# Layer 1's attention: the last tile's softmax weights made between the two halves of tile 1's value products, and stored and read ahead of the value loads

## The reference, cut to what matters

```python
x = x + jnp.tanh(g_xattn[1]) * _L1_xattn_ref(_layernorm(x, axis=-1), ctx_4096, ...)
# inside: C = 64 channels, 8 heads of depth 8, WINDOW = 16
# q, k, v = pointwise projections; for each t: softmax over 16 shifted keys of q.k / sqrt(8);
# out[t] = sum over the window of weight[t, w] * v[t + shift(w)]; then a pointwise projection
```

## Time and the profile before

| | us |
|---|---|
| median of 3 runs | 2050.9 |
| lowest and highest | 2050.52, 2055.03 |
| the profiled execution, its own time | 2056.09 |
| its span | 2053.9 |
| TensorE busy | 1871.9 (91%) |
| VectorE busy | 1630.7 (79%) |

### The profile page before, as it was taken

One profiled execution on the slowest core, in us unless ns is written; L12 is line 12 of the kernel. 1 busy time (PEld: TensorE's weight loads), 2 busy tenths in 40 slices (PEclk: granted clock), 3 DMA queues, 4 the chain that ended last, 5 costly groups with the idle time before them and its releaser, 6 DMA issues. The chain is left out here.

```text
span 2053.9 us, 37788 instructions
## 1 busy us (share of the span) xinstructions
PE 1871.9 (91%) x15015; PEld 1053.9 (51%) x15165; DVE 1630.7 (79%) x2908; ACT 585.7 (29%) x1347; POOL 655.3 (32%) x786
## 2 busy tenths in 40 slices
PE   8778989889889898998877999999999999999987
PEld 6434565446644456444533455555555555555543
DVE  4689776997679876797745888888888888888885
ACT  2322242223322233222333222222222222222443
POOL 3510242002420114202114544444343434343552
PEclk9899999999899998999988999999999999999997
DMA  8658204461055601463052111111111111111011
GB/s 246 186 157 229 68 2 145 124 190 57 2 165 155 195 2 42 130 195 89 2 179 77 42 32 52 52 52 48 51 42 52 52 52 52 52 32 32 16 37 52
DMA packets 142302, 176.52 MB, mean 86 GB/s; under 512 B 46769, under 2 KB 82769, under 8 KB 142001
## 3 DMA queue, kind: packets, MB, share of 16 engines
q1 hardware_dynamic: 140112, 172.88, 28.8%
q10 hardware_dynamic: 2016, 1.22, 0.3%
HBM read 131.98 MB, written 42.08 MB: 85 GB/s over the span
## 5 line engine op out<-in xcount | busy, mean ns | idle before, releaser
L1357 POOL TENSOR_TENSOR early_vare<-early_mv,w_eps 128x1 f32<-128x1 f32 x96 | 30.8, 321 | 748.3 <-DVE early_mv L1447 738.5
L2504 POOL TENSOR_TENSOR la_q<-la_straight,la_rot 128x512 f32<-128x512 f32 x128 | 163.0, 1273 | 160.3 <-DVE la_rot L2588 160.3
L441 PE MATMUL la_ps<-w_xTl,w_wqh 128*128 128x512 bf16 x512 | 196.8, 384 | 5.1 <-DVE la_rot L2588 3.8
L441 PE MATMUL la_ps<-w_wol,la_oTh 128*128 128x512 bf16 x512 | 194.0, 379 | 6.3
L440 PE MATMUL la_ps<-w_xTh,w_wqh 128*128 128x512 bf16 x505 | 194.9, 386 | 3.9 <-DVE la_rot L2588 3.8
L442 PE MATMUL la_ps<-w_xTh,w_wql 128*128 128x512 bf16 x510 | 195.4, 383 | 0.0
L442 PE MATMUL la_ps<-w_woh,la_oTl 128*128 128x512 bf16 x512 | 194.0, 379 | 0.0
L2517 POOL TENSOR_TENSOR la_p<-la_s,la_rec 128x256 f32<-128x256 f32 x128 | 89.6, 700 | 272.6 <-DVE la_rec L2609 269.9
L2434 ACT ACTIVATE la_oTh<-la_ps 128x256 bf16<-128x256 f32 x256 | 84.0, 380 | 295.0 <-PE la_ps L2317 295.0
L1607 DVE TENSOR_TENSOR early_products<-early_pR,early_vR 128x4096 f32<-128x4096 f32 x32 | 140.1, 4421 | 16.5 <-DMA early_pR<-scr_p 16.5
L440 PE MATMUL la_ps<-w_woh,la_oTh 128*128 128x512 bf16 x391 | 148.2, 379 | 0.0
(11 more groups left out here) (360 smaller groups left out, 4623.5 us busy)
## 6 DMA issues: line engine op xcount, KB each, us to landing
early_vR<-scr_v SPq DMA_DIRECT2D x128, 257.0 KB, 5.4
early_wkv<-wkv SPq DMA_DIRECT2D x32, 512.0 KB, 4.2
la_v<-v SPq DMA_DIRECT2D x64, 256.0 KB, 4.0
k<-early_ctxt SPq DMA_DIRECT2D x32, 256.0 KB, 3.9
v<-early_ctxt SPq DMA_DIRECT2D x64, 128.0 KB, 2.5
scr_p<-early_weights SPq DMA_DIRECT2D x16, 512.0 KB, 5.1
early_pR<-scr_p SPq DMA_DIRECT2D x32, 256.0 KB, 3.7
w_raw_q<-in_Wq SPq DMA_DIRECT2D x8, 1024.0 KB, 7.4
```

The costliest lines, as they stand in the source:

```text
L441: pe.matmul(out, lh[c], rl[c], start=False, stop=False)
L2504: rope_sum.send(pool.tensor_tensor(dst, straight[:, slot, :], rot[:, slot, :], ALU.add))
```

## The change

Four things change in each of the four turns.

- VectorE: `divide(3)` stands between the two halves of `times_values(1)`, no longer behind both.
- SyncE, tile 3: the weights' store, and the read of their first half, stand ahead of all eight value loads. The read of the second half stands between the two groups of four. Before, four loads came first, then the store, then four loads, then both reads.
- SyncE's waits for a free `vR` slot (tiles 2 and 3) are for VectorE's products (`pv_ready`) and no longer for TensorE's sum of them (`sum1`).
- SyncE's waits for a free `pR` slot are by halves, for the products of that half, and stand behind the wait for the store to land (`p1_written`).

```diff
-            def read_weights(turn, j):
-                if j >= 2:
-                    banks.wait_filled(sp, turn, "sum1", j - 2)
+            def read_weights(turn, j, halves=range(2)):
                 p1_written.wait(sp, turn, j)
-                for h in range(2):
+                for h in halves:
+                    if j >= 2:
+                        pv_ready.wait(sp, turn, 2 * (j - 2) + h)
                     src = scr_p[j, 0:1, h * TP:h * TP + 1]
...
-                banks.wait_filled(sp, turn, "sum1", 0)
+                pv_ready.wait(sp, turn, 1)
                 load_values(sp, turn, 2)
...
                 for f in range(10, 12):
                     keep_kv(turn, f)
-                banks.wait_filled(sp, turn, "sum1", 1)
+                write_weights(turn, 3)
+                read_weights(turn, 3, (0,))
+                pv_ready.wait(sp, turn, 3)
                 load_values(sp, turn, 3, range(CH // 2))
-                write_weights(turn, 3)
+                read_weights(turn, 3, (1,))
                 load_values(sp, turn, 3, range(CH // 2, CH))
-                read_weights(turn, 3)
...
-                def times_values(j):
+                def times_values(j, halves=range(2)):
                     p1_in[j % 2].wait(dve, turn, j // 2)
                     v_in[j % 2].wait(dve, turn, j // 2)
-                    for h in range(2):
+                    for h in halves:
...
-                times_values(1)
+                times_values(1, (0,))
                 divide(3)
+                times_values(1, (1,))
                 times_values(2)
                 times_values(3)
```

## The result

The changed kernel takes 2068.32 us in the median of 5 runs (2065.42 to 2072.17), the kernel before 2051.66 in the median of its 5 (2050.52 to 2055.03). The ratio is 1.0078, with a 95% interval of 1.0063 to 1.0094: slower by 16.7 us. The forecast was slower, by 7.3 us, with 2065.0 as the upper end. The sign holds, the size doesn't, and the interval leaves no room for mere spread.

A forecast was written before the change was run, and what follows sets the result against it. The prediction took VectorE's 16.5 us wait for tile 3's weights as all the change could win. TensorE's order (+2.9) and clock (+4.4) summed to +7.3 us, on 2050.9 giving 2058.2 us, range 2051.5 to 2065.0.

The forecast's parts named there:

- What ends the stall today, and what is late next: Before tile 3's products: a SyncE DMA chain ends today's 16.5 us stall; TensorE's queue, 3.65 us later, ends it next.
- The order alone, +2.9 us: Tile 3's products start later behind TensorE's queue: +2.6 us over four turns, with some 0.07 us each for handover, +2.9.
- The clock: Low TensorE clock behind the 4.2 us idle ahead of tile 1's second sum: 1.1 us a turn, bounds 0 and 1.72, +4.4.
- The spacing of the Trainium skill: 106.7 and 55.6 ns between matmuls: 48 wholly at the lower clock cost 2.45 us more, making the clock term 9.8.
- VectorE's own work unchanged: divide(3) between tile 1's halves only reorders VectorE's work; tile 2's products start at 434.4 as before: 0.
- the waits by `pv_ready` at nothing: SyncE's slot waits: tile 2's met one 1.9 us sum earlier but not waited for, tile 3's already met: 0.
- SyncE's new order, 448.0, hidden by TensorE: Tile 3's last value load, issued at 442.4, lands at 448.0 (bounds 443.8 to 450.1), before TensorE's 449.1.
- The rival by which the store's wait holds the loads: DMA decides tile 3's start at 450.1, +2.9 us a turn: +11.4, 2062.3 us; chance 0.15.
- The tail, 0: Behind tile 3's products the rest of the turn shifts by the same amount: 0, up to 0.5 us a turn if not.
- The signs: Expected profile: divide(3) about 4.4 us after tile 1's first product, TensorE idle 4.2, stall 5 to 6, loads from 15.5.

## Why the prediction was right in sign and wrong in size

- *What ends the stall today, and what is late next:* right. TensorE's in-order queue behind half 1 of tile 1's values took the DMA's place in all four turns. The shift of that half was put at 3.65 us. It was 3.82 (437.87 - 425.25 = 12.62, against 8.80).
- *The order alone, +2.9 us:* right as a bound. In the run with TensorE kept busy the buffer was free at 26.0, against 25.9 as worked out, with 11.55 us on the way where 11.56 was taken.
- *The clock, "I take 1.1", with 1.72 as its upper bound:* this is the step that failed. It measured 15.33 - 11.56 = 3.77 us in the second turn, some 15 us over four turns instead of 4.4. With 15.1 in its place the sum is 18.0 us, against 16.7 measured. The 1.72 came from one row, in which a low stretch of 3.4 us lay on projection 15. I carried over the length of the stretch from there. Here it was 10.2 us, and it covered the sum, the projection and part of projection 12. My argument that "a longer idle time lets part of the low stretch pass before work resumes" did happen, by 1.7 us (436.2 to 437.87), but it was small against a stretch three times as long. The length of the idle time doesn't explain this stretch by itself (last section).
- *The spacing of the Trainium skill ("TensorE: Matmul & The Clock Gate", "Wait — 56ns, not 53.3ns?"), as an estimate 9.8 for the term:* the measured 15 is above that, too. The spacing was not off: projection 15 of the kernel before, at the lower level, has its matmuls 0.11 us apart. What was off is the work taken to be slow: one projection, where it was a sum, tile 1's projection and part of projection 12.
- *VectorE's own work unchanged, the waits by `pv_ready` at nothing:* right for the order. For the waits, no run has the new order without them, so their 0 there is untested. By themselves they are worth a stall shorter by 3.7 us in the run that has only them, which I had missed because I had looked at their effect behind the new order alone.
- *SyncE's new order, 448.0, hidden by TensorE:* the loads started where they were put (15.3 instead of 15.5 us). The landing of the last one was mis-sized, a second failed term that TensorE's delay hid: up to 27.4 in the changed kernel and 28.6 with TensorE kept busy, where I had 25.9. I took the median of the group for its last member. The range of that row ended at 7.0, and 8.5 was measured. It didn't change the result, since TensorE was later still, as the run with SyncE's old order shows. But without any loss by the clock the change would still have cost the 9.9 us of the run with TensorE kept busy, more than the forecast's 7.3.
- *The rival by which the store's wait holds the loads:* right as a mechanism (the run with VectorE's old order has it alone, 1.0063), not what ended the stall in this result, where TensorE was later. The Trainium skill's rule ("DMA: Bandwidth & Descriptors", "Rules for kernel authors"), to issue early and wait late, agrees with that run: 28.1 us, against 24.1 with SyncE's old order.
- *The tail, 0:* the end shifted with the products. Some 7 us less lie outside the stretches in this pair of traces, but other pairs differ as much without a change there, so they show neither a gain nor a loss.
- *The signs:* `divide(3)` at 4.5 us, the idle time of 4.35 us, TensorE as the releaser and the loads at 15.3 us came as written. The stall of 8.8 us, ended by TensorE, was in neither list: I had no sign for a clock price above my bound.

## What to carry to other kernels

Before moving work between two halves on one engine, write out what another engine has queued in order behind the second half, and how long it will idle: that idle time can be paid twice, once as time and once in the clock of whatever is behind it. Don't carry over the length of a low clock stretch from one place to another. Where a wait has two chains that end within some 3 us of each other, removing one of them wins at most that difference, and a wait for a store to land belongs behind the loads that don't need it.

## What the runs showed of the hardware that I had not expected

- Behind an idle time of 4.3 us, ahead of float32 sums in narrow tiles, TensorE's granted clock was at 0.5 for 10.2 us in 8 of 8 turns; behind 2.3 us ahead of the same sums for 6.8 us in one turn and not at all in three. Behind 2.5 to 3.7 us ahead of a tile's projection and dense bfloat16 matmuls (the kernel before) it was there for 3.4 us. The other runs have longer idle times at that same place, ahead of tile 2's projection and projection 15: 4.0 to 4.8 us brought 3.4 us in eight turns and 6.8 in four (projection 12, or 12 and 13, between the sums), and 5.8 to 6.1 us brought 6.8 us in four of four (VectorE's old order). So the length of the idle time alone doesn't make the 10.2 us: in these stretches of layer 1's attention no dense work behind 4 to 6.5 us of idle time had more than 6.8. Why the sums have more stays open.
- 3.84 us of matmuls that nobody reads, in place of idle time, made the changed kernel about 7 us faster (9.9 over before instead of 16.7).
- The same eight loads of 257 KB, in the same order on SyncE, took at most 7.0 us to land in the changed kernel and 8.5 with TensorE kept busy. In the second the store of projection 12 followed the last load by 0.6 us, in the first by 3.0. That this store is the cause is not shown.
